# Second layer's attention: values as weights for four heads side by side, reciprocals turned on TensorE and multiplied in

## What is computed

```python
def _mha(query, key, value, Wq, bq, Wk, bk, Wv, bv, Wa, ba, mask=None):
    q = (query @ Wq + bq).reshape(Nq, Tq, NUM_HEADS, HEAD_DIM)
    k = (key @ Wk + bk).reshape(Nq, Tk, NUM_HEADS, HEAD_DIM)
    v = (value @ Wv + bv).reshape(Nq, Tk, NUM_HEADS, HEAD_DIM)
    attn = jnp.einsum('bthd,bshd->bhts', q, k) / np.sqrt(HEAD_DIM)
    if mask is not None:
        attn = jnp.where(mask == 0, -jnp.inf, attn)
    score = jax.nn.softmax(attn, axis=-1)
    y = jnp.einsum('bhts,bshd->bthd', score, v).reshape(Nq, Tq, D)
    return y @ Wa + ba
t2 = _mha(tgt, tgt, tgt, ..., tgt_mask)          # own attention
x = _layer_norm(tgt + t2, ln1_g, ln1_b)
t2 = _mha(x, memory, memory, ...)                # cross-attention, 375 keys
x = _layer_norm(x + t2, ln2_g, ln2_b)
t2 = jax.nn.relu(x @ lin1_W + lin1_b) @ lin2_W + lin2_b
return _layer_norm(x + t2, ln3_g, ln3_b)
```

## Time and profile before

| | us |
|---|---|
| median of 3 runs | 3834.25 |
| lowest, highest | 3819.92, 3880.32 |
| profiled execution | 3822.77 |
| its span | 3821.0 |
| PE busy in the span | 3584.9 (94%) |
| DVE busy | 2020.9 (53%) |
| ACT busy | 1746.1 (46%) |

### The profile page before, as it was taken

How to read it: one execution, slowest core, us unless ns; L and a number is a source line. 1 busy time by engine, 2 the same in 40 slices (tenths; PEclk the granted TensorE clock), 3 DMA queues, 4 the chain that set the end, 5 groups by cost and what they waited for, 6 DMA issues and landing times. The chain is left out here.

```text
span 3821.0 us, 67697 instructions
## 1 busy us (share of the span) xinstructions
PE 3584.9 (94%) x21748; PEld 2729.5 (71%) x21748; DVE 2020.9 (53%) x6215; ACT 1746.1 (46%) x4893; POOL 402.0 (11%) x488
## 2 busy tenths in 40 slices
PE   8999999999989999999997999999999997888888
PEld 6778778887867888888775666666676674565565
DVE  4644555464445555556554445445445445657656
ACT  3544545454443333334333545555555453344444
POOL 2101101110101111101101000000000001211111
PEclk9999999999999999999998999999999998898999
DMA  5000000000040000000001000000000000000000
GB/s 199 4 11 14 9 9 12 14 4 12 6 134 12 13 13 13 7 6 13 13 3 49 8 15 8 8 14 8 8 14 8 8 10 14 11 26 13 13 26 5
DMA packets 58462, 75.11 MB, mean 20 GB/s; under 512 B 6752, under 2 KB 55584, under 8 KB 57024
## 3 DMA queue, kind: packets, MB, share of 16 engines
q1 hardware_dynamic: 58176, 71.45, 5.9%
HBM read 64.04 MB, written 7.40 MB: 19 GB/s over the span
## 5 line engine op out<-in xcount | busy, mean ns | idle before, releaser
L161 PE MATMUL l_bank<-l_xT,weights_of_layers_and 128*128 128x224 f32 x2816 | 619.5, 374 | 17.2 <-ACT l_xT L1161 8.0
L161 PEld LDWEIGHTS l_bank<-l_xT,weights_of_layers_and 128*128 128x128 f32 x2816 | 550.1, 201 | 54.0 <-ACT l_xT L1161 8.7
L614 ACT ACTIVATE l_pT<-l_bank 125x336 f32<-125x336 f32 (+2 forms) x736 | 347.1, 472 | 341.0 <-PE l_bank L546 330.3
L546 PEld LDWEIGHTS l_bank<-identity,l_p 112*125 112x125 f32 (+2 forms) x2336 | 334.8, 178 | 184.6 <-issue 96.8
L546 PE MATMUL l_bank<-identity,l_p 112*125 112x112 f32 (+2 forms) x2336 | 390.0, 279 | 21.6 <-DVE l_p L590 18.2
L631 ACT ACTIVATE l_p<-l_p,l_nm 112x375 f32<-112x375 f32 x384 | 233.4, 608 | 284.9 <-DVE l_nm L665 283.8
L161 PE MATMUL l_bank<-l_cT,weights_of_layers_and 128*128 128x375 f32 x832 | 306.3, 495 | 4.7 <-DVE l_z L1811 3.7
L161 PE MATMUL l_bank<-weights_of_layers_and,l_cT 128*125 128x256 f32 (+2 forms) x960 | 301.0, 451 | 0.2
L728 POOL TENSOR_TENSOR l_ve<-l_mv,eps 112x2 f32<-112x2 f32 (+1 forms) x89 | 17.3, 195 | 2548.7 <-DVE l_mv L722 2548.7
L590 DVE TENSOR_SCALAR l_p<-l_p,l_rs 112x375 f32<-112x375 f32 (+1 forms) x608 | 255.1, 420 | 21.7
L568 PEld LDWEIGHTS l_bank<-l_pT,l_cv 125*64 125x64 f32 (+1 forms) x3648 | 163.6, 131 | 138.7 <-issue 98.7
(11 more groups left out here) (253 smaller groups left out, 6118.6 us busy)
## 6 DMA issues: line engine op xcount, KB each, us to landing
l_cT<-in_ctx_turned SPq DMA_DIRECT2D x32, 375.0 KB, 3.4
l_cx<-in_ctx SPq DMA_DIRECT2D x16, 375.0 KB
context_rows<-in_ctx_reversed SPq DMA_DIRECT2D x16, 375.0 KB
tokens<-x_after_layer SPq DMA_DIRECT2D x25, 224.0 KB, 2.6
x_after_layer<-l_z SPq DMA_DIRECT2D x24, 224.0 KB, 2.4
weights_of_layers_and<-bias_lines_kept SPq DMA_DIRECT2D x1, 2625.0 KB, 16.3
weights_of_layers_and<-in_L_xattn_w_fused SPq DMA_DIRECT2D x1, 2048.0 KB, 10.7
weights_of_layers_and<-in_L_xattn_w_ff SPq DMA_DIRECT2D x1, 2048.0 KB, 12.7
```

The lines of the kernel that those rows point to most:

```text
L161: last = pe.matmul(out, left, right, start=(k == 0), stop=(k == len(pairs) - 1))
L546: last = pe.transpose(TR.bank(m)[:ph.keys, g * ph.rows:(g + 1) * ph.rows], p[:ph.rows, m % self.p_slots, g * ph.keys:(g + 1) * ph.keys], i ...
L614: return act.activation(out, src, ACT.Copy)
```

## The change

The second layer gets a class of its own, Quarters (its predecessors Phase and Attention's methods go, since no other layer used them).

- Values and probabilities change places: the values of a head are the weights, 32 columns (two heads' width, of which 16 are zeros), and the transposed probabilities move, 112 columns. Four heads go to the four quarters of the output's partitions, in one burst: 3 tiles x 4 heads for cross, after every fourth item; 4 heads for own, for each item. A head and its neighbour are added into the same quarter by a second burst, each with zeros in the other's place. The output of a batch (16 heads) stands turned, features on partitions, in one bank (bank 4, ring O), and its transposes cOT and OT go.
- The sums are no 17th column any more. For cross, exp writes them (accum_out); for own, VectorE sums the probabilities (totals). Once per batch and attention VectorE takes the reciprocals, each repeated 16 times (spread, 112x256); PE turns them in two transposes into the other half of bank 4; VectorE copies them out and multiplies.
- Cross queries are spread over four heads instead of eight. Score products take the low or the high 64 partitions of keys and queries. The order of the heads is changed to fit. Own scores keep 128 partitions.
- Scores have 2 banks, transposed probabilities 2, output 1; ring P keeps its 3 for the chain and side work, without the outputs.
- Transposes lag by 3 items, values by 4, and PE does transposes before scores in a step. The copies of cross's transposed probabilities go to ScalarE and VectorE in turn.
- v and cv are cleared as a whole at the layer's start by POOL (768 elements to a partition in v, 2304 in cv, instead of 32 and 96), ahead of what PE and ScalarE wait for.

```diff
-class Phase:
...
+class Quarters(Attention):
...
+        self.spread = sb("spread", T, H, 16)
...
+        def scores(ph, k):
+            m = ph.first + k
+            for sem, count in S.free(i, m, *ph.ready(k)):
+                pe.wait_ge(sem, count)
+            width = ph.keys * ph.tiles
+            for g in range(ph.n):
+                last = pe.matmul(S.bank(m)[:T, g * width:(g + 1) * width], ph.q(k, g), ph.k(k, g), start=True, stop=True)
+            last.then_inc(S.full.sem, 1)
...
+        def values(ph, k):
+            if not ph.bursts(k):
+                return
+            m = ph.first + k
+            job, column, half = ph.place(k)
+            together = [k] * 4 if ph.grouped else list(range(k - 3, k + 1))
+            ready = [TR.got(ph.first + n) for n in together] + ph.val_ready(k)
+            for sem, count in O.free(i, job, *ready) if ph.opens(k) else counts(i, *ready):
+                pe.wait_ge(sem, count)
+            for t in range(ph.tiles):
+                for a, n in enumerate(together):
+                    at = a if ph.grouped else t
+                    last = pe.matmul(O.bank(job)[32 * a:32 * a + 32, column:column + T], ph.val(n, a, t),
+                                     pT[:ph.keys, (ph.first + n) % self.pT_slots, at * T:(at + 1) * T],
+                                     start=(t == 0 and half == 0), stop=(t == ph.tiles - 1 and half == 1))
+            if ph.closes(k):
+                d = ph.job0 + O.index[job] - O.index[ph.output_jobs()[0][0]]
+                pe.wait_ge(self.spread_laid.sem, self.spread_laid.count(i, 2 * d))
+                for t in range(KT):
+                    last = pe.transpose(O.bank(job)[:, TP + t * T:TP + (t + 1) * T],
+                                        self.spread[:, t * 8:(t + 1) * 8, :].rearrange("p h e -> p (h e)"), ident[:T, :T])
+                last.then_inc(O.full.sem, 1)
+            else:
+                last.then_inc(self.values.sem, 1)
+
+        self.lagged(parts, [(self.lag_t, turns), (0, scores), (self.lag_v, values)], between)
...
+                act.activation(slot[:, 0:S2], S.bank(m)[:T, 0:S2], ACT.Exp, bias=nm[:, n, k:k + 1], accum_out=sums[:, n, j, h:h + 1]).then_inc(S.emptier(m).sem, 1)
...
+        def totals(ph, k):
+            m, n = ph.first + k, self.phases.index(ph)
+            j, h = ph.head(k, 0)
+            if ph.grouped:
+                dve.wait_ge(self.probs.sem, self.probs.count(i, ph.probs0 + k))
+                own = sums[:, n, j, h:h + 8].rearrange("p (a b) -> p a b", b=2)[:, :, 0] if h % 2 == 0 else sums[:, n, j, h - 1:h + 7].rearrange("p (a b) -> p a b", b=2)[:, :, 1]
+                dve.tensor_reduce(own, p[:, m % self.p_slots, :].rearrange("p (g t) -> p g t", g=G), AX.X, ALU.add).then_inc(self.summed.sem, 1)
+            if ph.closes(k):
+                if ph.grouped:
+                    dve.wait_ge(self.summed.sem, self.summed.count(i, ph.summed0 + k))
+                else:
+                    dve.wait_ge(S.emptier(m).sem, S.count_emptied(i, m))
+                dve.reciprocal(self.spread[:, :, :], wide(sums[:, n, j, :], 2, 16)).then_inc(self.spread_laid.sem, 1)
+
+        def turned(ph, k):
+            if ph.turned_by(k) == "dve":
+                self.turned_copy(dve, i, ph, k, lambda out, src: dve.tensor_copy(out, src))
+
+        def outputs(ph, k):
+            if ph.closes(k):
+                job = ph.place(k)[0]
+                dve.wait_ge(O.full.sem, O.count_full(i, job))
+                bank = O.bank(job)
+                dve.tensor_copy(ph.out(k), bank[:, TP:2 * TP].rearrange("p (t x) -> p t x", t=KT)).then_inc(self.spread_laid.sem, 1)
+                dve.wait_ge(self.spread_laid.sem, self.spread_laid.count(i, 2 * (ph.job0 + ph.head(k, 0)[0]) + 1))
+                dve.tensor_tensor(ph.out(k), bank[:, 0:TP].rearrange("p (t x) -> p t x", t=KT), ph.out(k), ALU.mult).then_inc(O.emptier(job).sem, 1)
+
+        self.lagged(parts, [(self.lag_t, turned), (0, maxima), (0, amid), (1, totals), (self.lag_v, outputs)], between, amid)
...
-        qz, qz_own = sb("qz", 128, KT, HEADS_PER_TILE, TP), sb("qz_own", 128, KT, HEADS_PER_TILE, TP)
-        v, cv = sb("v", T, PAIR, H, DH + 1), sb("cv", CP, PAIR, CT, H, DH + 1)
+        qz, qz_own = sb("qz", 128, KT, HALF, TP), sb("qz_own", 128, KT, HEADS_PER_TILE, TP)
+        v, cv = sb("v", T, PAIR, H // 2, 3 * DH), sb("cv", CP, PAIR, CT, H // 2, 3 * DH)
+        LAG_VALUES = 4
...
+        def cross_head(k, g):
+            n = k % H
+            return k // H, n // 8 * 8 + n % 4 * 2 + n % 8 // 4
...
+        def half_of(a, h):
+            n = h % 8 // HALF * 64
+            return a[n:n + 64, :]
...
+        def cross_query(k, g):
+            j, h = cross_head(k, g)
+            return half_of(qz[:, h // 8, h % HALF, j * T:(j + 1) * T], h)
...
+        def value(a, h):
+            return a[:, h // 2, h % 2 * DH:h % 2 * DH + 2 * DH]
...
+                     sides=4, turned_by=lambda k: "dve" if k % 2 else "act")
...
-        A = Attention(ctx, nc, "l1", [cross, own], banks[0:3], banks[3:5], P)
+        O = Ring(ctx, nc, "l1_output", banks[4:5], cross.output_jobs() + own.output_jobs())
+        A = Quarters(ctx, nc, "l1", [cross, own], banks[0:2], banks[2:4], O, 3, LAG_VALUES, 4, 6)
...
-            for a in (v[:, :, :, DH:], cv[:, :, :, :, DH:]):
-                pool.memset(a, 1.0).then_inc(zeroed, 1)
+            for a in (z[:, :, :], v[:, :, :, :], cv[:, :, :, :, :]):
+                pool.memset(a, 0.0).then_inc(zeroed, 1)
...
-                    for sem, count in P.free(i, f"{name}{j}", P.got(turned)):
+                    for sem, count in P.free(i, f"{name}{j}", turned(j)):
-                    turn_tokens(pe, c, P, i, "cOT", A.O, P.got(cross.output_jobs()[-1][0]))
+                    attend(i, "u", V["ca"], lambda j: O.got(f"cO{j}"))
-                turn_tokens(pe, c, P, i, "OT", own.out, P.got_before(own.output_jobs()[-1][0]))
+                attend(i, "y", V["sa"], lambda j: O.got_before(f"sO{j}"))
...
-                dve.scalar_tensor_tensor(qz[:, t, :, :], wide(P.bank(name)[:, 0:TP], 1, HEADS_PER_TILE), bias[:, t:t + 1],
+                dve.scalar_tensor_tensor(qz[:, t, :, :], wide(P.bank(name)[:, 0:TP], 1, HALF), bias[:, t:t + 1],
```

More of the change, by code:

```diff
@@ L423, in signals @@
-    def signals(self):
-        return [self.neg_max, self.probs, self.values]
 class Part:
@@ L1467, in layer1 @@
[L1467 to L1471 removed]
+            return [P.got(f"cv{k // H}1")] if k % H == 3 else []
@@ L1472, in layer1 @@
+        cross = Part("c", PAIR * H, DH, T, cross_query, cross_key,
+                     lambda k, g, t: value(cv[:, cross_head(k, 0)[0], t], cross_head(k, 0)[1]), cross_ready, cross_values_ready,
+                     lambda k: place(f"cO{k // H}", k % H // 4), lambda k: OT[:, :, k // H * T:(k // H + 1) * T],
+                     sides=4, turned_by=lambda k: "dve" if k % 2 else "act")
+        own.head, cross.head = own_head, cross_head
         OWN = cross.items
-        ENDS = OWN + own.items + LAG_V
```

438 lines of the change are left out of this document (177 added, 261 removed), and 2 rows, old and new, of the table P.

## The result

The change is slower. Median 4035.7 us (4031.4 to 4038.3, 4 runs) against 3857.3 us (3819.9 to 3882.4, 4 runs) of the kernel before beside it: ratio 1.054, 95% interval 1.051 to 1.058. The kernel before comes at two levels of time, here 3820 and 3834 us against 3880 and 3882, and the ratio is taken from the lower pair. The profiled execution took 4033.4 us, its span is 4031.6 us, 210.6 more than before. The forecast of 3828 us, and its range up to 3880, are wrong.

What follows compares the result with a forecast made beforehand. PE, busy 94% of the span, was taken as the bound, losing time to the clock in own attention. Seven turns +4, last turn -3, first pass +1, layer's start 2.5: together +5 on 3822.8, so 3828 us, range 3755 to 3880.

Steps and rivals of the forecast that it cites:

- Burst, item, divisions: Cross-attention on PE: value burst 0.71 us for four heads, transposes plus score 1.30 us, division changes 0.36 us of that.
- Rival 1: Cross-attention: scores in half of the rows cost nothing extra, 1.28 us a head, 3775 us in all; chance 0.16.
- The cross stretch: The 32 cross-attention scores of a turn, to the first of own attention: 47.0 us against 48.7, so -1.7 us.
- The clock in cross-attention: Cross-attention was taken as granted the full clock, as in the trace of before.
- Rival 3: Clock falls in cross-attention too, from half-row products with drained engine; a third of the stretch, +12 us a turn, 3924; chance 0.09.
- Its head at the low level: Cross-attention in the slower rival: a head's 1.48 us of PE becomes some 2.6 us at the low clock level.
- Own attention: Own attention with its side work: VectorE comes onto the path, 47 us against 43.7, +3.3 us a turn.
- The 6 us added for a longer low clock: Own attention: half of the hidden layer and what follows lies in the low clock, adding 6 us a turn.
- the working's own 41 us: Own attention before the low-clock addition: hidden layer starts at 24.7 us, then PE sets the pace, 41 us in all.
- Rival 4: Own attention is no slower, since what idles at the low clock would have idled anyway; 7 x -3.3, 3805 us; chance 0.15.
- Reciprocals and sums: VectorE: reciprocals of 112x256 take 1.93 us, or 0.43 if they stream; sums of own probabilities 0.62 us a group.
- Chain, first pass, start of the layer: Chain: -0.4 us for transposes, -0.56 for the first score's wait; first pass VectorE-paced, +1; POOL's clearing at the start, some 2.5.

Runs made afterwards that it cites:

- a: The kernel after the change with cross queries spread over eight heads again, so scores contract over all 128 partitions; 3760.2 us, ratio 0.984.
- c: On a, each score product split over the array's columns, 64 and 48 of the 112 queries, all rows used; 3800.1 us, one run.
- i: The kernel after the change with three banks for scores and two for the chain; 3830.2 us, one run.
- k: The kernel after the change with two banks for chain and side work instead of three, one bank unused; 3836.3 us, ratio 1.000.
- j: On a, the first eight scores of each turn contract over 64 partitions, the other 24 over 128; 3823.9 us, one run.
- l: The same kernel as i, timed in 10 runs; 3830.6 us, ratio 0.995.

## Why the prediction was wrong, point by point

- **Burst, item, divisions: right at the full clock.** A burst is 0.71 us, as forecast. An item is 0.51 + 0.81 = 1.32 us (forecast 1.30), against 0.95 with full rows in a. The changes of division cost 0.37 a score (forecast 0.36); c, another pair of divisions, 0.33. Rival 1 (half rows cost nothing extra) is false. The cross stretch is 47.2 us (47.0). The Trainium skill says that a change of the tiling mode drains the engine (TensorEngine Tiling (Array Packing), Key Properties). The measured 0.37 and 0.33 us agree with it.
- **The clock in cross-attention: the step that failed.** The sum took the full clock there as given, because the earlier trace rows have it at 1.00 and the bursts of the earlier trace rows keep it. Neither holds a product in half of the rows. Measured: 82 us instead of 47 in seven of eight turns. Against before that is 6 x 33.6 = 201.6 us in the full turns and 28.9 from the last turn's first cross score to the end, 230.5 together; all else gave 19.9 back, which leaves the 210.6. Rival 3 named the fall and the products in half of the rows, but it erred twice. It let a third of the stretch be low, where it was nearly all: in none of the low stretches of half-row scores alone did the clock come back before they ended. And it named the drained array around each product as part of the cause, where c shows that changes of division over columns alone leave the clock up, but for pieces of 3.4 to 6.8 us. Its head at the low level, 2.6 us, is near what the rows give: four heads take 3 x 2.42 + 3.70 = 10.96, so 2.74 each; and half a microsecond lost for each one at the low level (9.5 of 19) is near the measured 34.9 (82.1 less 47.2) for 77.6. With the whole stretch in place of a third, in the seven turns in which it fell, it would have said 3828 + 7 x 36 = 4080 us. The third and the chance of 0.09 were chosen, and no row of before excluded the rest.
- **Own attention: wrong sign.** Forecast 47 us against 43.7, measured 41.9. The order of events was right: the hidden layer starts 24.6 us behind the first own score (forecast 24.7), PE waits for VectorE's output there in every turn, 15 times and 22.6 us in the layer, 1.9 at most:

```profile
  PE l_bank L571: 22.6, 15
```

  The 6 us added for a longer low clock were wrong. The waits are longer than before, but the low pieces behind them are 3.4 to 6.8 us, against 10.3 to 13.7 before, and the hidden layer's first half takes 4.8 us from its start to the next instruction's, against 5.9 before. Without the 6 the working's own 41 us is 0.9 from the measured. Rival 4 had the outcome right, that own attention is no slower; no run shows that its reason is the one.
- **Reciprocals and sums.** 112x256 take 1.75 us, by the group of after below, against 1.93 forecast and 0.43 if they streamed; sums 0.61 (0.62). The Trainium skill says that the reciprocal divides iteratively, with a repeat count of 8 (VectorE: DVE Perf Modes, First, the fixed hardware budget). That is the right direction, but the estimate made from it, 2.1 us and a fixed part, is over the measured 1.75.

```profile
L645 DVE RECIPROCAL l_spread<-l_sums 112x256 f32<-112x256 f32 x32 | 55.9, 1748 | 0.6
L639 DVE TENSOR_REDUCE l_sums<-l_p 112x4 f32<-112x448 f32 x64 | 39.1, 610 | 0.4
```

- **Chain, first pass, start of the layer.** The chain lost 1.1 us (0.4 for the transposes and 0.56 for the first score's wait were forecast). The first pass was called VectorE-paced and +1: from its first own score to the first cross score it takes 42.6 us where before took 49.9, so -7.3. POOL's clearing and preparing takes 4.1 us instead of 1.4, and the first own score stands 1.9 us further behind the start of that (2.5 forecast).
- **The sum.** An estimate of the time with the clock up in cross-attention takes 34.9 us off for each of the seven low stretches: 4033 - 244 = 3789 us. i and k, with one fall each, come near it: 3830 - 34 = 3796 and 3836 - 34 = 3802. So the change would have been about 1% faster than before, and the clock puts it 6% above that. The 3789 is 39 below the forecast, mostly for own attention's sign (41.9 against 47 in seven turns, 36 us) and the first pass (8), less the smaller terms that came out worse. So the error in own attention hid some 40 us of what the clock cost.

What is open: what picks the turns in which the clock falls. It fell, at the starts, 3 to 5 us behind the first score; equal starts had both outcomes; neither the score's wait nor an earlier low piece decides it. A start moved by fixed small steps, with nothing else changed, was not tried. Nor were the scores of two heads run in the two halves at once, so that no rows stand idle.

## What to carry to other kernels

A product over half of the array's rows costs the same columns and, at the full clock, 0.37 us more here for changing the array's division; the larger price is that a stretch made of such scores can lose the full clock, and in no run here did it come back before they ended. Before making operands narrower to save memory, look for a buffer that is idle at the time: here that turned 5% slower into 2% faster with one bank moved as well, and 3.5% with VectorE's chain in own attention shortened. And price a rival whose mechanism the trace can't exclude over the whole stretch it could reach, not over a share chosen for it.

## What the runs showed of the hardware

- Once the clock has fallen, a stretch of half-row scores stays at 1.2 GHz to its end with PE busy for 77.6 of 77.6 us; full-row scores bring 2.4 GHz back 1.5 to 3.3 us behind the first of them (j). Where it hasn't fallen, the same half-row scores run at 2.4 GHz through a whole stretch (seven of eight in i, k and l).
- The same instructions have two outcomes: 47 or 82 us for one cross-attention. Between kernels that differ in a bank that the scores don't use, the count of low ones in the trace went from seven to one and the time from 4036 to 3836 us.
- Two column tiles of one score run side by side: 0.77 us for 64 and 48 columns together (c), against 0.63 for one product of 112 columns without a change of division.
- A reciprocal of 112x256 takes 1.75 us, of 112x16 0.25, a copy that spreads 112x16 to 112x256 0.29.
